# Direct sums by source for 60 instead of 20 of every 125 edge columns, with split float32r weights and a 1664-wide one-hot

## The reference

```python
x = _layernorm(x + gat(x))        # two attention layers: softmax over dst, 3 heads and 1 head
x = _layernorm(x + gcn(x))        # two convolutions: sum over dst of h[src] * norm
x = _layernorm(x + sheaf(x))      # below
x = _layernorm(x + product(x))    # below
# sheaf: per edge, two 16-vectors from a small MLP of (x[src], x[dst]) give reflections F_s, F_d
out = x - zeros.at[src].add(msg_s) - zeros.at[dst].add(msg_d)
# product: per edge, silu(x[dst] (outer) edge_attr, times W) summed over `row` = src
agg = segment_sum(m @ W_msg_lin, row)
```

## Time and profile before

| | us |
|---|---|
| median of 3 runs | 39,602.82 |
| lowest, highest run | 39,334.77, 39,683.62 |
| the profiled execution, its span | 39,946.08, 39,944.3 |
| busy in the span: PE, weight loads, DVE, ACT, POOL | 14,169.2, 10,724.1, 16,251.5, 2,594.5, 21,803.8 |

### The profile page before, as it was taken

The page is one execution under the profiler, slowest core; times in us unless marked ns, Lnnn a source line. Parts: engine busy times, 40 slices in busy tenths (PEclk is TensorE's granted clock), DMA queues, the critical chain, the costliest instruction groups (busy, mean ns, idle before and its releaser), DMA issues. The chain is left out here.

```text
span 39944.3 us, 271822 instructions
## 1 busy us (share of the span) xinstructions
PE 14169.2 (35%) x71326; PEld 10724.1 (27%) x71326; DVE 16251.5 (41%) x34865; ACT 2594.5 (6%) x3901; POOL 21803.8 (55%) x20450
## 2 busy tenths in 40 slices
PE   1111100111111036665566533423433343166664
PEld 1000000100000035554455412212222222144443
DVE  2333337222222546665566522323332332344443
ACT  0000000000000000000000000000000000033331
POOL 4655640455455246664676555564455555377773
PEclk5555555555555567776787756656666666577775
DMA  2000013111111211111111110000000000100001
GB/s 43 13 12 11 13 9 123 15 18 18 17 20 18 95 37 29 28 28 20 25 29 29 23 10 9 11 10 8 8 11 9 9 11 8 50 16 14 14 14 47
DMA packets 1088987, 932.94 MB, mean 23 GB/s; under 512 B 580668, under 2 KB 1031892, under 8 KB 1063892
## 3 DMA queue, kind: packets, MB, share of 16 engines
q1 hardware_dynamic: 440100, 695.25, 5.8%
q0 software_dynamic: 646368, 201.76, 5.3%
q10 hardware_dynamic: 1872, 28.29, 0.2%
HBM read 497.08 MB, written 426.83 MB: 23 GB/s over the span
## 5 line engine op out<-in xcount | busy, mean ns | idle before, releaser
L1100 POOL DMA_INDIRECT messages<-se_M,se_rstage x2625 | 2951.3, 1124 | 4001.5 <-DVE se_M L1463 3209.2
L1100 POOL DMA_INDIRECT messages<-pe_M,pe_rstage x2625 | 3129.7, 1192 | 1097.5 <-issue 792.2
L493 POOL DMA_INDIRECT g1g_G<-tab,g1g_stage x3125 | 3130.6, 1002 | 1038.0 <-issue 1021.1
L493 POOL DMA_INDIRECT se_G<-tab,se_stage x3125 | 3016.8, 965 | 1038.9 <-issue 1026.0
L493 POOL DMA_INDIRECT g2g_G<-tab,g2g_stage x3125 | 2953.3, 945 | 1041.0 <-issue 1022.0
L999 DVE SCALAR_TENSOR_TENSOR g2gh_junk<-g2gh_pB,g2gh_src_f,earlier 128x128 f32<-128x128 f32 (+4 forms) x2625 | 1453.8, 614 | 3827.6 <-remote 3062.9
L1408 DVE TENSOR_TENSOR se_V<-se_pTV,s_b 128x160 f32 (+1 forms) x625 | 202.7, 324 | 6708.2 <-remote 3856.6
L493 POOL DMA_INDIRECT c2c_G<-tab16b,c2c_stage x2125 | 2567.2, 1208 | 659.0 <-issue 640.0
L493 POOL DMA_INDIRECT c1c_G<-tab,c1c_stage x2125 | 2549.1, 1200 | 658.9 <-issue 641.5
L1011 PE MATMUL g2gh_pB<-ident_b,src_lo 128*128 128x128 bf16 x2625 | 665.1, 286 | 5191.0 <-issue 3725.7
L711 PE MATMUL g1gh_acc<-g1gh_oh_hi,g1gh_oh_lo 128*128 128x100 bf16 x6250 | 634.1, 284 | 4733.2 <-DVE g1gh_oh_hi L692 2182.6
(11 more groups left out here) (594 smaller groups left out, 34505.6 us busy)
## 6 DMA issues: line engine op xcount, KB each, us to landing
scans<-g1w_W SPq DMA_DIRECT2D x25, 3187.5 KB, 9.9
c1cm_row<-match SPq DMA_DIRECT2D x500, 128.0 KB
c2cm_row<-match SPq DMA_DIRECT2D x500, 128.0 KB
edges<-g2g_G SPq DMA_DIRECT2D x25, 2062.5 KB, 6.4
g2w_G<-edges SPq DMA_DIRECT2D x25, 2062.5 KB, 11.6
scans<-g2w_W SPq DMA_DIRECT2D x25, 2062.5 KB, 7.3
g1g_G<-tab,g1g_stage POOLq DMA_INDIRECT x3125
g2g_G<-tab,g2g_stage POOLq DMA_INDIRECT x3125
```

The costliest lines, as they stand in the source:

```text
L493: g.indirect_dma_start(out=G[b][:, t, :], out_offset=None, in_=table, in_offset=bass.IndirectOffsetOnAxis(ap=stage[b][:, t:t + 1], axis=0) ...
L1100: g.indirect_dma_start(out=view, in_=M[b][:, DC + t, :], in_offset=None, out_offset=bass.IndirectOffsetOnAxis(ap=stage[b][:, t:t + 1], axis=0)
```

## The change

`DG` goes from 4 to 12, so 60 columns of a chunk are summed directly and 65 are sent. `count_in_group` has 13 groups in a chunk, `count_before_group` 7 and 6.

One direct column is made differently. The sum is kept transposed: 128 rows are 8 node tiles x 16 features, and 1664 = 13 x 128 columns are the rest of the node number. DVE compares a float16 ramp of 1664 with one number for each edge (`hot`, float32r) and multiplies an 8-wide one-hot with the message, split into a rounded part and its rest (`spot`, 2 x 8 x 16 = 256). PE takes each of the two `spot` tiles as weights against four pieces of `hot`, 416 wide: eight float32r matmuls, one record each. `prepare` makes what the columns of a chunk share, with eight chained DVE instructions, in the sheaf after `messaged`, in the product before the direct columns. In the sheaf the 60 columns of chunk i - 1 ride three by three in steps 1 to 20, made and used in the same step. In the product 13 groups go first without direct columns, then 12 groups with five each. At each stage's end the sum is turned back with 13 transposes. Tiles are moved to smaller scopes to make room.

```diff
-DG = 4
+DG = 12
 DC = DG * GRP
...
 class DirectSums:
...
     def products(self, pe, b, start):
-        for q in range(self.BANKS):
-            mm = pe.matmul(self.acc[:, q, 0:self.w * D], self.oh_lo[b][:, :],
-                           self.wide[b][:, q * self.w:(q + 1) * self.w, :].rearrange("p t d -> p (t d)"),
-                           start=start, stop=True, skip_group_check=True)
+        for n in range(PARTS):
+            for q in range(self.BANKS):
+                mm = pe.matmul(self.acc[:, q, 0:self.w], self.spot[b][:, n, :, :].rearrange("p r f -> p (r f)"),
+                               self.hot[b][:, q * self.w:(q + 1) * self.w],
+                               start=start and n == 0, stop=True, skip_group_check=True)
         mm.then_inc(self.added, 1)
-    def vector(self, v, k, M, i, d, b):
+    PREPARED = 8
+    def prepare(self, v, ch, M, i):
+        k = self.k
+        at = bass.ds(i * CH, DC)
+        values = M[:, 0:DC, 0:D]
+        ch(v.tensor_copy(self.part[:, :, 0, :], values))
+        ch(v.tensor_tensor(self.part[:, :, 1, :], values, self.part[:, :, 0, :], ALU.subtract))
+        ch(v.tensor_scalar(self.slot_i[:, :], k.src_i[:, at], 7, MR - 1, ALU.logical_shift_right, ALU.bitwise_and))
+        ch(v.tensor_copy(self.slot[:, :], self.slot_i[:, :]))
+        ch(v.tensor_tensor(self.slot_hot[:, :, :], bc(self.slot[:, :], [P, DC, MR], 2),
+                           bc(k.iota[:, 0:MR], [P, DC, MR], 1), ALU.is_equal))
+        ch(v.tensor_tensor(self.row[:, :], k.src_hi[:, at], self.slot[:, :], ALU.subtract))
+        ch(v.tensor_scalar(self.row[:, :], self.row[:, :], float(P // MR), None, ALU.mult))
+        ch(v.tensor_tensor(self.row[:, :], self.row[:, :], k.src_lo[:, at], ALU.add))
+    def vector(self, v, i, d, b):
         m = i * DC + d
-        at = bass.ds(i * CH + d, 1)
+        at = bass.ds(d, 1)
         v.wait_ge(self.added, m + 1)
-        v.tensor_tensor(self.oh_lo[b][:, :], k.iota[:, :], k.src_lo[:, at].to_broadcast([P, P]),
+        v.tensor_scalar(self.hot[b][:, :], self.count[:, :], self.row[:, at], None,
                         ALU.is_equal).then_inc(self.made, 1)
-        v.tensor_tensor(self.oh_hi[b][:, :], k.iota[:, 0:NT], k.src_hi[:, at].to_broadcast([P, NT]),
-                        ALU.is_equal).then_inc(self.hot, 1)
-        v.wait_ge(self.hot, m + 5)
-        v.tensor_tensor(self.wide[b][:, :, :], bc(self.oh_hi[b][:, :], [P, NT, D], 2),
-                        M[:, bass.ds(d, 1), 0:D].to_broadcast([P, NT, D]), ALU.mult).then_inc(self.made, 1)
+        shape = [P, PARTS, MR, D]
+        v.tensor_tensor(self.spot[b][:, :, :, :],
+                        self.slot_hot[:, at, :].unsqueeze(3).to_broadcast(shape),
+                        self.part[:, at, :, :].rearrange("p a n f -> p (a n) f").unsqueeze(2).to_broadcast(shape),
+                        ALU.mult).then_inc(self.made, 1)
     def tensor(self, pe, i, d, b):
         pe.wait_ge(self.made, (i * DC + d) * 2 + 2)
...
+            v.tensor_copy(self.total[:, q * self.w:(q + 1) * self.w],
+                          self.acc[:, q, 0:self.w]).then_inc(self.moved, 1)
+        v.wait_ge(self.turned, 1)
+        for j in range(MJ):
+            n = min(MR, NT - j * MR)
+            v.tensor_copy(out[:, j * MR:j * MR + n, :].rearrange("p r f -> p (r f)"),
+                          self.acc[:, j // 4, (j % 4) * P:(j % 4) * P + n * D]).then_inc(self.out_sem, 1)
+    def tensor_last(self, pe):
+        pe.wait_ge(self.moved, self.BANKS)
+        for j in range(MJ):
+            mm = pe.transpose(self.acc[:, j // 4, (j % 4) * P:(j % 4 + 1) * P], self.total[:, j * P:(j + 1) * P],
+                              self.k.ident[:, :])
+        mm.then_inc(self.turned, 1)
...
+ROUNDS, STEPS, PER_STEP = 5, 4, (3, 3, 3, 3)
+def direct_columns(m, n):
+    start = sum(PER_STEP[0:n])
+    return [(m * sum(PER_STEP) + d, d % 2) for d in range(start, start + PER_STEP[n])]
+assert ROUNDS * sum(PER_STEP) == DC and sum(PER_STEP) % 2 == 0 and ROUNDS * STEPS < NG - 1
...
-                    def spread_column(d, half):
-                        if direct_before:
-                            sums.vector(v, k, M[1 - b], i - 1, d, half)
-                    def group_step(q, half=None):
+                    def group_step(q, direct=()):
                         v.wait_ge(transposed, i * NG + q + 1)
                         pair_group(q + 1)
                         v.wait_ge(evacuated, i * NG + q)
                         group_dots(q - 1)
-                        if half is not None:
-                            spread_column(q, half)
+                        for d, half in direct:
+                            sums.vector(v, i - 1, d, half)
                         evacuate(q)
                     pair_group(0)
                     v.wait_ge(transposed, i * NG + 1)
                     pair_group(1)
-                    spread_column(0, 0)
                     evacuate(0)
-                    with v.Fori(0, DC // 2 - 1) as m:
-                        ch.enter(m, 10)
-                        group_step(2 * m + 1, 1)
-                        group_step(2 * m + 2, 0)
-                        ch.leave(DC // 2 - 1, 10)
-                    group_step(DC - 1, 1)
-                    with v.Fori(DC, NG - 1) as q:
-                        ch.enter(q - DC, 5)
+                    with v.Fori(0, ROUNDS) as m:
+                        ch.enter(m, 5 * STEPS)
+                        for n in range(STEPS):
+                            group_step(STEPS * m + (n + 1), direct_columns(m, n) if direct_before else ())
+                        ch.leave(ROUNDS, 5 * STEPS)
+                    for q in range(ROUNDS * STEPS + 1, NG - 1):
                         group_step(q)
...
-                    if direct_before:
-                        v.wait_ge(sums.made, i * (2 * DC))
                     A = T[:, :, 0, :]
                     v.wait_ge(mfree[b], j + 1)
                     take_off(A, X[b][:, :, 0:D], 1, dots[:, :, 3])
                     reflect(A, A, 0)
                     ch(v.tensor_tensor(M[b][:, :, 0:D], A, bc(X[b][:, :, D], [P, CH, D], 2), ALU.mult))
                     v.tensor_copy(M[b][:, :, D], k.src_i[:, cols(i)]).then_inc(messaged, 1)
+                    if direct_before:
+                        v.wait_ge(sums.made, i * (2 * DC))
+                    sums.prepare(v, ch, M[b], i)
...
-                    def group_step(q, d=None, half=0):
+                    def group_step(q, direct=()):
                         hidden_layer(i * NG + q)
                         transpose(i * NG + q + 1)
-                        if d is not None:
+                        for d, half in direct:
                             sums.tensor(pe, i - 1, d, half)
                         pe.wait_ge(copied, i * NG + q + 2)
...
-                    with v.Fori(0, DC // 2) as m:
-                        outer_products(2 * m + (DG + 1))
-                        sums.vector(v, k, M[b], i, 2 * m, 0)
-                        outer_products(2 * m + (DG + 2))
-                        sums.vector(v, k, M[b], i, 2 * m + 1, 1)
+                    v.wait_ge(sums.made, i * (2 * DC))
+                    sums.prepare(v, ch, M[b], i)
+                    v.nop(nofuse=True)
+                    with v.Fori(0, DG // 2) as m:
+                        for half in range(2):
+                            outer_products(2 * m + (DG + 1 + half))
+                            for d in range(half * GRP, (half + 1) * GRP):
+                                sums.vector(v, i, 2 * GRP * m + d, d % 2)
                     v.wait_ge(sums.made, (i + 1) * (2 * DC))
```

121 lines of the change are left out of this document (67 added, 54 removed).

## The result

Beside the kernel before on the same chip, the changed kernel takes 0.9881 of its time (95% interval 0.9849 to 0.9913): a gain of 1.2%, some 470 us, where I forecast +0.1%. Medians of all twenty runs are 39,436.66 us against 39,688.63, 0.6% apart (the ratio leaves disturbed runs out, and runs of the changed kernel spread over 2.7%). The profiled execution has a span of 39,747.3 us against 39,944.3: -197, where my sum said +70. What the runs gained beyond them is not in this pair of profiles, and where it lies is open.

What follows compares the result with a forecast made beforehand. It took PE's signals, stuck at 2.8 us a record while POOL issues, to set the pace of three stages, and POOL to bound the product. Terms -940, -250, -70, +830, +500 sum to +70; forecast 39,650 us, range 36,700 to 41,200.

Steps and rivals of the forecast that it cites:

- my sum: Whole kernel: all stage terms together +70 us on 39,946, less than the measurement can tell; chance 0.40.
- Small parts: Clearing, turning back and one more stage +30 us; columns at the sheaf's end beside POOL's shorter last scatter -30.
- Product: Product stage: POOL stops bounding it, the groups form the path, 202 us a chunk, +830 us.
- the sheaf: Sheaf stage: 57 us less POOL time, but fewer groups done while stuck and dearer groups after, +500 us.
- the convolutions: Both convolutions: four count groups fewer a chunk, about 150 us a chunk, -250 us together.
- The attention gather: Second attention layer: eight count groups that ran after POOL stopped go, 4.70 us each, -940 us.
- The scans: Source-order scans: 65 columns instead of 105, a fifth off each of two, -70 us.
- A direct column: Sheaf and product: one column takes 1.5 us on DVE (compare 1.1, `spot` 0.4) and 1.6 on PE.
- rival D: Wide compare runs at L1290's slower rate, so DVE leads in product and sheaf: +1,900 us, 41,600; chance 0.10.
- A: Sheaf's stall goes: 313 us a chunk, -2,850 us, whole 36,400 to 36,900; chance 0.25, a third of it partial.
- B: Convolutions become POOL-bound at 132 us a chunk: -1,100 us instead of -250, whole 38,800; chance 0.10.
- C: Convolutions' stall takes the last four steps, not one: 182 us a chunk, +1,200 us, whole 41,100; chance 0.15.

Runs made afterwards that it cites:

- chips 7 and 4: Changed kernel against the kernel before, repeated on two other chips with the stall: ratio 1.0157 on chip 7, 1.0107 on chip 4.
- chips 6 and 15: Changed kernel against the kernel before on two chips without the stall: 1.0216 on chip 6; 1.0222 on chip 15, there with empty instructions on POOL.

## Why the prediction was wrong, point by point

**The sign.** My sum said +70 us and the pair of profiles shows -197: 267 us apart, less than 0.7% of the time, but with the wrong sign (the runs as a whole gained more, some 470). Two steps failed. *Small parts*, "60 columns at the sheaf's end run beside POOL's last scatter, which is 57 us shorter: -30": the rows of the two ends show -162 in all. I looked at the sheaf's end only, and halved it; in both stages DVE and PE had finished 65 to 85 us before POOL's last issue, so a shorter scatter shortens the path there one for one until they end together. *Product*, 202 us a chunk against 197.1 measured, +830 against +725:

```profile
36038.79 0.83 DVE L1755 TENSOR_TENSOR pe_outer<-pe_X,pe_A 128x640 f32 x1 [3.43 <-PE pe_pT L1786]
36043.05 0.83 DVE L1755 TENSOR_TENSOR pe_outer<-pe_X,pe_A 128x640 f32 x1 [3.43 <-PE pe_pT L1786]
...
36111.10 0.82 DVE L1755 TENSOR_TENSOR pe_outer<-pe_X,pe_A 128x640 f32 x1
...
36121.00 0.82 DVE L1755 TENSOR_TENSOR pe_outer<-pe_X,pe_A 128x640 f32 x1
```

The thirteen groups without columns, at 4.26 us in one chunk and 6.04 in the next, take 57 and 78 us with the wait and `prepare`, 67.7 on average, for which I had 63 + 9 = 72; and a group with five columns takes 9.90 us, not 10.1 (12 x 0.2 = 2.4). The 63 was also worked out wrong: thirteen groups at 4.7 and 6.0 in turn make 70. And the kernel before's 169 us a chunk, which I put down to POOL alone, had 10 us of stall in it. The forecast of +33 a chunk wasn't hurt by that, since it started from the measured 169.

These two steps are 263 of the 267 us; the sheaf's -32 and the convolutions' +28 cancel.

**Right with its cause.** The attention gather: -935 against -940, eight groups at 4.7 us that ran after POOL had stopped. The scans' -70 against -77 (the fifth was a guess). A direct column: DVE's compare took 1.10 to 1.12 us (1.1), `spot` 0.42 (0.4), so rival D is out.

**Right by luck.** The sheaf: +468 against +500, but not as I had it. I let every step be stuck at 120 us while POOL issues, with four of 25 done at its end; in the first profile steps took 12 us even beside POOL for much of the time, one or two were stuck, and about nine were done at its end. Against that a free step took 12.0 us, not 11: PE's 24 column records wait 2 us for DVE and then run at a low clock. The two errors cancelled. There is a third: 496 against 461 in two thirds of the chunks and 464 against 444 in the others make +30 a chunk, 750 us, not my +21 and +500; summed rightly my forecast would have been +320. On chips 7 and 4, where the stall comes almost at once as I had it, the stage took 12,658 and 12,683 us, above my upper bound of +1,200. The convolutions' -222 against -250 is no better than luck, since one code varies by more.

**The rivals.** A (the stall goes, 313 us a chunk) is what chips 6 and 15 show, at 332 us; but there it goes from the kernel before too, which A didn't reckon with, and the change is 2.2% slower. B's 132 us for a convolution chunk is the measured pace there (3,312/25 = 132.5). In the first profile, from one start of POOL's gather to the next, 37 of 48 convolution chunks took 109 to 157 us, half of them 136 or less, near B; the other eleven took 207 to 229, with DVE idle for 50 us and more in the middle of a chunk where I looked: a stall that comes early, as in C, and dearer. Their mean is near my 150 by that mixture.

**The frame.** It didn't cause the miss of the first pair, but the larger error is that I took the stall of one profile for a property of the kernel. It is a property of the kernel on a chip: the same code takes 4,018 or 5,885 us in the attention gather. Of the two rules of the Trainium skill that I weighed, "TensorE: Matmul & The Clock Gate", section "The cost: per-tile semaphore tail", has about 26 ns for an increment. That is compatible with chips 6 and 15, where a group follows in 4.7 us, and not with a stuck group's 28.0 us on the others; I had held it refuted.

## What to carry to other kernels

Before a prediction rests on a stall, look whether it is there on another chip: here a change worth 1.2% on one chip cost 1.1 to 2.2% on four others (on one of them measured with empty instructions on POOL), while work made one step ahead and columns spread over all groups made it 6 to 8% faster than the kernel before on two chips with the stall; without the stall that wasn't measured by itself. A work-splitting change pays only where the engine it relieves sets the pace; read the ends of stages for that too. Where one engine makes operands for PE in the same step, making the first one a step early can remove more than the wait: here PE's clock rose with it.
